# Sparsemax attention in a decoder kernel: VectorE takes the candidates' differences, GpSimd the flags

## The reference

```python
def sparsemax(x):
    x = x - jnp.max(x, axis=-1, keepdims=True)
    zs = -jnp.sort(-x, axis=-1)
    rho = jnp.arange(1, L + 1, dtype=x.dtype)
    cssv = jnp.cumsum(zs, axis=-1) - 1.0
    support = zs > cssv / rho
    k = jnp.maximum(jnp.sum(support, axis=-1, keepdims=True), 1)
    tau = jnp.take_along_axis(cssv, k - 1, axis=-1) / k.astype(x.dtype)
    return jnp.clip(x - tau, 0.0)
```

## Time and profile before

| | us |
|---|---|
| median of 3 runs | 3807.26 (3803.86 to 3811.04) |
| profiled execution, its own time | 3801.61 |
| its span, first to last instruction | 3799.9 |
| PE busy | 3021.0 (80%) |
| DVE busy | 2351.3 (62%) |
| ACT busy | 2099.1 (55%) |
| POOL busy | 1442.6 (38%) |

### The profile page before, as it was taken

One profiled execution on the slowest core, in us unless ns is written; L12 is line 12 of the kernel. 1 busy time (PEld: TensorE's weight loads), 2 busy tenths in 40 slices (PEclk: granted clock), 3 DMA queues, 4 the chain that ended last, 5 costly groups with the idle time before them and its releaser, 6 DMA issues. The chain is left out here.

```text
span 3799.9 us, 68257 instructions
## 1 busy us (share of the span) xinstructions
PE 3021.0 (80%) x21678; PEld 1815.0 (48%) x21678; DVE 2351.3 (62%) x10231; ACT 2099.1 (55%) x6518; POOL 1442.6 (38%) x2225
## 2 busy tenths in 40 slices
PE   8999996999999824888867888888888875878782
PEld 4555553666666622444434445444444443444441
DVE  2445553666666685666649999999999963111112
ACT  3323221666666602777738998989989871222110
POOL 0222222555555545555524444454444440110005
PEclk9999997999999966888868898898889875999996
DMA  1000001111111011000010000000000005116773
GB/s 68 19 20 16 16 14 43 41 39 42 40 42 39 22 40 54 22 24 24 23 41 19 18 23 20 23 18 21 23 18 23 20 5 196 36 63 224 232 236 115
DMA packets 112064, 192.06 MB, mean 51 GB/s; under 512 B 11150, under 2 KB 95886, under 8 KB 105550
## 3 DMA queue, kind: packets, MB, share of 16 engines
q1 hardware_dynamic: 102094, 166.32, 13.8%
q10 hardware_dynamic: 7200, 14.68, 1.0%
q0 software_dynamic: 2400, 6.56, 0.5%
HBM read 149.90 MB, written 37.62 MB: 49 GB/s over the span
## 5 line engine op out<-in xcount | busy, mean ns | idle before, releaser
L3063 DVE MAX8 sa_cand<-sa_s 128x8 f32<-128x45 f32 (+3 forms) x3328 | 399.2, 189 | 31.2 <-ACT sa_s L2909 31.2
L699 POOL TENSOR_SCALAR ca_p<-ca_p,ca_rec 100x361 f32<-100x361 f32 x512 | 284.4, 575 | 328.5 <-DVE ca_rec L977 328.5
L879 ACT ACTIVATE ca_p<-ca_sm,ca_nb 100x361 f32<-100x361 f32 x512 | 301.7, 591 | 190.6 <-DVE ca_nb L963 182.6
L2668 POOL TENSOR_SCALAR sa_s<-sa_s,sa_unit,sa_nu 128x361 f32<-128x361 f32 (+1 forms) x416 | 261.6, 647 | 204.0 <-DVE sa_nu L3155 204.0
L2792 PE MATMUL sa_tr<-sa_ident,sa_s 128*128 128x128 f32 (+3 forms) x1248 | 232.1, 306 | 113.2 <-ACT sa_pT L2943 99.2
L963 DVE CUSTOM_DVE_ANT_0 ca_sm<-ca_sc,ca_mb 100x361 f32<-100x361 f32 x512 | 251.7, 524 | 53.5 <-PE ca_sc L786 53.5
L2925 ACT ACTIVATE sa_spare_a<-sa_s,sa_nu 128x361 bf16<-128x361 f32 (+1 forms) x416 | 247.3, 596 | 56.3 <-DVE sa_nu L3157 56.3
L2917 ACT ACTIVATE sa_s<-sa_s,sa_nt 128x361 f32<-128x361 f32 (+1 forms) x416 | 248.1, 608 | 23.6 <-DVE sa_nt L3116 23.3
L2792 PEld LDWEIGHTS sa_tr<-sa_ident,sa_s 128*128 128x128 f32 (+3 forms) x1248 | 165.7, 161 | 183.2 <-ACT sa_pT L2943 128.2
L2658 POOL TENSOR_TENSOR sa_over<-sa_cand,sa_tc 128x280 f32<-128x280 f32 (+3 forms) x128 | 99.5, 778 | 400.8 <-DVE sa_tc L3082 263.3
L2778 PE MATMUL sa_sc<-sa_kT,sa_qm 32*128 32x361 f32 (+3 forms) x768 | 228.2, 523 | 23.0 <-ACT sa_s L2909 22.3
(11 more groups left out here) (319 smaller groups left out, 7377.3 us busy)
## 6 DMA issues: line engine op xcount, KB each, us to landing
ea_we<-m_experts SPq DMA_DIRECT2D x40, 1024.0 KB, 6.7
ea_wd<-m_experts SPq DMA_DIRECT2D x40, 512.0 KB
ca_cTs<-cT SPq DMA_DIRECT2D x32, 361.0 KB
sa_cTs<-cT SPq DMA_DIRECT2D x32, 361.0 KB
rows_in<-me_zeros ACTq DMA_DIRECT2D x1, 7168.0 KB
ea_xe<-rows_in SPq DMA_DIRECT2D x40, 128.0 KB
rows_out<-ea_ye ACTq DMA_DIRECT2D x40, 128.0 KB
ca_ms<-mask SPq DMA_DIRECT2D x32, 141.0 KB
```

The lines of the kernel that those rows point to most:

```text
L699: ins = pool.tensor_scalar(p[:, r, j, :], p[:, r, j, :], rec[:, r, j:j + 1], 1.0, ALU.mult, ALU.mult)
L879: act.activation(p[:, r, j, :], sm[:, r % 2, j, :], ACT.Exp, bias=nb[:, r % 2, j:j + 1], scale=-1.0, accum_out=den[:, r, j:j + 1]).then_in ...
L2668: pool.tensor_scalar(s[0:rows, u, i, :], s[0:rows, u, i, :], unit[0:rows, :], nu2[0:rows, i:i + 1], ALU.mult, ALU.add).then_inc(p_done.sem, 1)
L3063: ins = dve.max(cand[0:rows, i, q, :], s[0:rows, u, i, PART[q]:PART[q + 1]])
```

## The change

For each refinement GpSimd still subtracts, now into slot 1 of `over`, waits for its own result, and turns it in place into flags, signalled by the new `flag_done`. VectorE makes the same differences itself into slot 0 (`gap`), on the signal `tc_done`, waits, cuts them at 0, waits, sums slot 0, waits for `flag_done`, and sums slot 1. The steps that one group's two refinements count rise from 14 to 16.

```diff
+        flag_done = Event(a, "flag_done", 4)
...
-        CAND_STEPS = 14
+        CAND_STEPS = 16
...
-                pool.tensor_tensor(over[g][:, :, 0, 0:8 * w].rearrange("p t (q l) -> p t q l", l=w), cand[:, ts, :, 0:w],
+                flags = over[g][:, :, 1, 0:8 * w]
+                pool.tensor_tensor(flags.rearrange("p t (q l) -> p t q l", l=w), cand[:, ts, :, 0:w],
                                    tc[:, ts].unsqueeze(2).unsqueeze(3).to_broadcast([P, tiles, 8, w]),
                                    ALU.subtract).then_inc(less_done.sem, 1)
+                pool.wait_ge(*less_done.at(n, 2 * g + k + 1))
+                pool.tensor_scalar(flags, flags, 0.0, None, ALU.is_gt).then_inc(flag_done.sem, 1)
...
+            def gap(g, ts, w):
+
+                tiles = ts.stop - ts.start
+                return dve.tensor_tensor(over[g][:, :, 0, 0:8 * w].rearrange("p t (q l) -> p t q l", l=w),
+                                         cand[:, ts, :, 0:w],
+                                         tc[:, ts].unsqueeze(2).unsqueeze(3).to_broadcast([P, tiles, 8, w]), ALU.subtract)
...
                 if j == 0:
-                    dve.wait_ge(*less_done.at(n, 2 * g + k + 1))
-                    chain.count(dve.tensor_scalar(over[g][:, :, 1, 0:nc_k], over[g][:, :, 0, 0:nc_k], 0.0, None, ALU.is_gt))
-                    chain.count(dve.tensor_scalar(over[g][:, :, 0, 0:nc_k], over[g][:, :, 0, 0:nc_k], 0.0, None, ALU.max))
+                    dve.wait_ge(*tc_done.at(n, 2 * g + k + 1))
+                    chain.then(gap(g, ts, FIRST_L if k == 0 else 8))
+                    chain.then(dve.tensor_scalar(over[g][:, :, 0, 0:nc_k], over[g][:, :, 0, 0:nc_k], 0.0, None, ALU.max))
                 if j == 1:
-                    chain.wait()
-                    chain.count(dve.tensor_reduce(both[:, ts, :], over[g][:, :, :, 0:nc_k], AX.X, ALU.add))
+                    chain.count(dve.tensor_reduce(both[:, ts, 0], over[g][:, :, 0, 0:nc_k], AX.X, ALU.add))
+                    dve.wait_ge(*flag_done.at(n, 2 * g + k + 1))
+                    chain.count(dve.tensor_reduce(both[:, ts, 1], over[g][:, :, 1, 0:nc_k], AX.X, ALU.add))
```

More of the change, by code:

```diff
@@ L2634, in _ @@
         def _(pool):
-            open_all(pool, qm_done, less_done, p_done, xb_done, xn_done)
+            open_all(pool, qm_done, less_done, flag_done, p_done, xb_done, xn_done)
             identity(pool, ident, setup, 0)
```

## The result

The changed kernel takes 3851.53 us (median of 4 runs, 3851.06 to 3852.0), the kernel before 3805.82 us beside it (3803.86 to 3811.04): ratio 1.012, 95% interval 1.0105 to 1.0134. It is slower by 45.7 us.

The account below looks back on a forecast made before the run. VectorE's written order was taken to bound the sparsemax stage. Refinement changes of +0.25, +0.52, -0.05 and +0.49 us sum to +1.21 per sequence, times 32 +39 us, giving 3846 us (range 3818 to 3872).

Parts of the forecast that it names:

- Gap's own price and its hold: VectorE's gap: 0.40, 0.44, 0.55, 0.62 us for 240, 280, 384, 448 elements per partition, held by GpSimd's subtraction except in 280.
- The order in 448: Refinement with 448 elements per partition: gap waits from 0.42 to 0.88 us for GpSimd's subtraction; reciprocal at 3.48, +0.52 us.
- rival 1: GpSimd's subtraction does not hold VectorE's gap, since both only read: -17 us, 3790 us; chance 0.07.
- Flags on GpSimd: GpSimd's flags take 0.4 to 0.6 us alone; their streaming, 0.23 to 0.42 us, holds VectorE's positive part.
- The wait on the flags: VectorE's wait for GpSimd's flags before the second sum is already open, with 0.5 us to spare.
- 280: Refinement with 280 elements per partition: gap before flags, reciprocal at 2.81 us, +0.49; flags first, 2.98, +0.66.
- GpSimd's delay: GpSimd's steps behind its flags come some 0.9 us later; its waits for nu, 3.2 us each, cover that.
- Norm: The norm's small operations slide to a place beside VectorE's 7-element steps: 0 to 8 us, taken as 0.
- Sum: The four refinements add 1.21 us per sequence, times 32: +39 us, with no VectorE idle time to hide it.
- Rival 2: Gap is held, but VectorE's positive part gets in ahead of GpSimd's flags: +13 us, 3820 us; chance 0.11.
- rival 4: The shared port is held to the reported end throughout: 39 + 31, 3877 us; chance 0.04.
- rival 3: GpSimd holds VectorE longer: bias add passes positive part in 384 (+22 us) or flags stream slower (+24); about 3869; chance 0.13.

Follow-up runs that it names:

- idle subtraction: Changed kernel with VectorE doing the refinements alone, plus GpSimd subtracting into a tile nobody reads: 3867.02 us, ratio 1.0164 to the kernel before.
- exchanged counts: Changed kernel with tiles 11 and 12 swapped in the second count: 3836.04 us, ratio 1.0077 to the kernel before.
- half count: Changed kernel with tiles 11 and 12 swapped in the second count and tile 11's on 64 partitions only: 10870.99 us, the sublayer being computed once more.
- the run with the flags alone: Kernel before with only the flags moved to GpSimd, made from its own differences, and two separate sums on VectorE: 3814.09 us, ratio 1.0024.

## Why the prediction came out, step by step

**Bound.** Right: VectorE's written order sets the stage, and nearly all of the 50 us by which the stage grew are found in its refinements (48 us pass by pass).

**Gap's own price and its hold.** Right in 240 and 384. There the gap ends 0.40 and 0.55 us after the compare's data, which are done 0.13 to 0.14 us before the reported end; the idle subtraction shows that no signal makes it wait. The Trainium skill ("SBUF — State Buffer", Who interferes with whom) has the conflict, and the runs bear it out for two SBUF inputs; its "whole instruction" they don't, if the reported end is the end: by those 0.13 us, and by more in the flags below.

**The order in 448: the step that failed.** I had gap wait for the compare from 0.42 to 0.88. It passed it, as rival 1 has it, but rival 1's gain did not follow: the compare became 0.82 us longer, held the positive part to 1.70 (0.14 before its end) and put the flags off to 1.93. Reciprocal 3.95 for 3.48: 0.47 us times 32, 15 us. The exchanged counts give 3.41 back, the half count 3.94.

**Flags on GpSimd: mis-sized.** Predicted 0.4 to 0.6 us, measured 0.86 to 1.35. What holds VectorE, though, is only their first part. The 240 refinement of the changed kernel (T = 2554.20):

```profile
2554.62 0.55 DVE L3080 TENSOR_TENSOR sa_over<-sa_cand,sa_tc 128x240 f32<-128x240 f32 x1
...
2555.00 0.86 POOL L2664 TENSOR_SCALAR sa_over<-sa_over 128x240 f32<-128x240 f32 x1
...
2555.20 0.35 DVE L3104 TENSOR_SCALAR sa_over<-sa_over 128x240 f32<-128x240 f32 x1
```

In 240 the positive part took 0.35 us for its 0.28 and ended at 1.36, so, with its own length taken off, it really began near 1.07, 0.27 after the flags' start and 0.59 before their end; in 384 near 1.55, 0.54 after and 0.81 before. I had 0.23 and 0.36 of streaming. The mis-sized length therefore cost little where the second sum came late enough, and in both forms the positive part ended 0.04 us, the reciprocal came 0.06 us sooner than predicted.

**The wait on the flags.** The 0.5 us to spare were not there. In 240 and 384 the second sum starts 0.05 us after the flags' end, just without a wait, and in 448 it waits 0.52, 16.6 us over the stage: flags twice as long, begun late.

**280.** Here the flags got in first (T = 2535.06):

```profile
2535.95 0.91 POOL L2664 TENSOR_SCALAR sa_over<-sa_over 128x280 f32<-128x280 f32 x1
...
2536.06 0.61 DVE L3080 TENSOR_TENSOR sa_over<-sa_cand,sa_tc 128x280 f32<-128x280 f32 x1
```

They start at 0.89, the gap at 1.00; the gap took 0.61 for its 0.42, and the positive part then hardly waited (0.33 for its 0.31). The forecast had the other order as the likelier, and for this one 2.98. That the reciprocal comes at 2.84, within 0.03 us of the 2.81 forecast, is luck.

**GpSimd's delay.** Right: its wait for nu fell from 193.6 to 111.9 us, and nothing of VectorE waits for the probabilities.

**Norm.** Taken at 0; the 7-element step gives 2.3 us back, a gain instead of the loss of 0 to 8, because the norm's last operation was put off past it.

**Sum.** 39 predicted; 448 adds 15, the other three forms take 3 off, the small step 2: 49 by medians of the passes. That the time came within 6 us of the prediction thus rests on the mechanism, which the experiments bear out, and in part on luck: errors in the terms that partly cancel. Rival 2 falls (where the gap was held, the positive part was never ahead of the flags); so does rival 4 (gap's record is 0.55 us in 240, not 0.69). Of rival 3 the bias add falls (L2679 starts behind the positive part); the flags do hold longer than forecast, 0.54 us in 384, but from 1.01 on, and so let the positive part end 0.04 us earlier.

## What to carry to other kernels

Before elementwise work is split between VectorE and GpSimd, reckon with the two lengths added rather than with the longer. In these runs a VectorE step with two inputs in SBUF, or a plain tensor_scalar, and a GpSimd operation held each other, and the wait stood inside the held instruction's own record, where no view of waits shows it. The sums were not held: half a sum in 448 took 0.62 us beside the flags and 0.62 after them. Look for an instruction whose mean is far above that of its like on as many elements, and see what GpSimd runs beside it; moving such a filler (the bias add) and one small VectorE step (the product) to other places was worth 0.7% here. And an operation taken away from GpSimd moves the one behind it forward: see whom it meets there.

## What was not expected of the hardware

- Flags ("above 0") on GpSimd, in the run with the flags alone, take 0.91 us for 240 and for 280 elements and 1.33 us for 384 and for 448: two levels, not a slope, over these four sizes. Subtractions on the same tiles take 0.63, 0.71, 0.83 and 0.94.
- In 448, with a VectorE instruction on 64 partitions right ahead, the two-input one passes a GpSimd subtraction begun 0.34 us earlier (which grows from 0.94 to 1.75 us); with one on 128 partitions ahead it is held. The mechanism is open.
- A product of 7 elements, 0.19 us in its later place, lost 0.4 us beside GpSimd's two masked copies and 1.0 us when a bias add followed them.
